# First attention of a Flamingo block: 16-bit planes of the probabilities transposed by DMA, split by GpSimd and joined by ScalarE

## The chip, the cores and the metric

One core of a Trainium2 chip runs the whole program. The metric is the device time of one execution in microseconds; lower is better.

## What is computed

The reference is a residual stack of four cross-attention layers and four feed-forward layers on `x` of 4 x 256 tokens x 256 features: Mamba, dense FFN, **first attention**, sparse experts, second attention, experts, quantised experts, chosen tokens. All of it is float32. The change concerns the first attention (the reference's `_L1_xattn_ref`), which for each of 4 batches and 16 heads of width 128 is

```
q = rms(xn @ Wq) * gq        # 256 x 128
k = rms(ctx @ Wk) * gk       # 256 x 128
p = softmax(q @ k.T / sqrt(128))      # 256 x 256
x = x + tanh(g) * (p @ (ctx @ Wv)) @ Wo
```

## The kernel before, in words

Every engine has its own program, written out in order; they meet at semaphores (`wait_ge`). The names used below are those of the code. The stages follow each other, and generators called `beside` put pieces of the next stage into a running one (`step(beside[...])`).

The first attention (`attention1_pe`, `_act`, `_dve`, `_pool`) runs over 64 **units**: unit u is one head of one batch. Units come in 32 **passes** N = u // 2, one head for two batches; passes 0 to 15 are the 16 heads for batches 0 and 1, 16 to 31 those for batches 2 and 3. The values are not projected: `a1_joined_pe` makes M = Wv Wo of a head once, the unit multiplies the probabilities with the raw context (`attend`), and then with M (`result`). K of passes 0 to 15 was projected earlier, during Mamba, so passes N below 16 project only Q.

For unit u TensorE does, in its own iteration u:

- `scores(u + 1)`, four 128 x 256 matmuls in two banks' halves (L1257; float32 matmuls appear as several records);
- in an even iteration `a1_turn_pe` for pass N + 1, eight transposes of Q and K (L1095);
- `transposed(u)`: four 128 x 128 transposes of the probabilities into PSUM bank 2 or 3 (L1268);
- even: `a1_project_pe` for K of pass N + 3 (L1074, from N + 3 = 16 on); odd, while N + 3 is below 16: `a1_joined_pe` (L1084);
- `attend(u - 1)` (L1277); even: the projection of Q (L1071); `result(u - 2)` (L1288).

ScalarE, in iteration u: scales the turned Q and K (L1131, even); waits for the transposes `a1_T` and copies them from PSUM to `PT` (L1343); squares or copies K's projection (L1107; L1115, L1116) or M (L1121); `exponentials(u + 1)` into `Pr`, two halves with their sums (L1331); squares and copies Q's projection (L1115, L1116). VectorE: the maxima of unit u + 1 (L1365, L1368), the inverse of the sums (L1374), the product copied to `Z` (L1380), the residual of `result` (L1389), then normalisation (L1155, L1158) or the sums of squares (L1142, L1144). GpSimd has one inverse root a pass (`a1_root_pool`, L1167), and in the second half the indirect scatters of the sorted experts' tokens (L1742), two at a step.

SP issues the loads: each pass's weights of 384 KB into one of two buffers (`attention1_sp`, L1053), and, between those of pass 19 and 20, the small tables and the 6 MB of weights of the sorted experts (`sorted_first_sp`, L1526 to L1531) and the second attention's weights (`a2_first_sp`). After the last pass's weights it goes on to the sorted experts' row loads (L1543).

The buffers matter for the waits. `Pr`, `PT` and `Z` have two places each, so work on unit u waits for the reader of unit u - 2:

```
        act.wait_ge(*at("a1_T", u))
        if u >= 2:
            act.wait_ge(*at("a1_A", u - 2))
        nc.scalar.copy(m.PT[:, w, :, :],
                       bank[2 + w].rearrange("p (t d) -> p t d", t=2)).then_inc(*tick("a1_PT", u))
```

## Time and profile before

| | us |
|---|---|
| median of 3 runs | 1067.0 (1062.03 to 1067.75) |
| the profiled execution, its own time | 1065.21 |
| its span, first to last instruction | 1063.9 |
| PE busy | 947.4 (89%) |
| DVE busy | 724.5 (68%) |
| ACT busy | 521.4 (49%) |
| POOL busy | 303.0 (28%) |
| mean granted TensorE clock | 0.947 of full speed |

The median and the profiled execution are different runs of the same program. Busy time is the union of an engine's instructions; waiting, semaphores and the issue of DMAs are not in it. PE is the row of matmuls and transposes, PEld that of weight loads, which overlap the matmuls; the first attention's units run from about 220 to 552 us of the span.

### The profile page before, as it was taken

What the parts mean: (1) busy time and instruction counts of PE and PEld (TensorE: products, weight loads), DVE (VectorE), ACT (ScalarE), POOL (GpSimd) and SP (SyncE); (2) the same over time, 40 slices, a digit from 0 to 9 for tenths busy, and PEclk for the clock granted to TensorE, in tenths of its full rate; (3) what the DMA queues carried; (4) which work ended last, traced back from release to release, by engine and by line L of the source; (5) the groups of instructions that cost most, each with busy time, mean ns of one, the idle gap of its engine ahead of it and who ended that gap; (6) DMA issues with size and microseconds to landing.
All of it is one profiled execution on the core that took longest, in us unless ns stands there. A gap on an engine that the chain in (4) does not pass through costs nothing.

```text
span 1063.9 us, 14909 instructions
## 1 busy us (share of the span) xinstructions
PE 947.4 (89%) x4814; PEld 678.0 (64%) x4814; DVE 724.5 (68%) x1877; ACT 521.4 (49%) x1346; POOL 303.0 (28%) x284
## 2 busy tenths in 40 slices
PE   7878789999999999999999989877788889988587
PEld 3323334567999998888977767754455546545475
DVE  5899894235777677678676445678798855667753
ACT  4665672135666666566644434354366542132331
POOL 3667692121111112155101424244312100011110
PEclk9888999999999999999999999999799999989689
DMA  9500001011111164122103436411100004202100
GB/s 362 227 0 0 1 0 50 1 30 44 35 43 46 45 231 156 31 66 90 45 1 119 160 119 198 129 65 51 50 1 2 1 3 156 75 31 61 55 20 20
DMA packets 28500, 75.00 MB, mean 70 GB/s; under 512 B 4092, under 2 KB 5382, under 8 KB 27656
## 3 DMA queue, kind: packets, MB, share of 16 engines
q1 hardware_dynamic: 24344, 63.81, 17.6%
q0 software_dynamic: 3072, 8.39, 2.5%
q10 hardware_dynamic: 1008, 1.86, 0.6%
q8 instruction: 39, 0.64, 0.3%
q14 instruction: 37, 0.30, 0.1%
HBM read 52.03 MB, written 22.02 MB: 70 GB/s over the span
## 4 chain that ended last, share of the span: by engine, by line
PE 63%; DVE 15%; issue 3%; ACT 2%; DMA 1%; SPq 1%; POOL 1%; DVEq 0%; POOLq 0%; ACTq 0%
PE psum L2195 5%; PE psum L1071 5%; PE psum L1796 5%; PE psum L1277 4%; PE psum L1288 4%; PE psum L927 4%; PE psum L1257 4%; PE psum L1268 2%; PE psum L938 2%; PE psum L2458 2%; PE psum L2816 2%; PE psum L1810 2%; PE psum L1095 2%; PE psum L2214 2%; PE psum L2834 2%
## 5 line engine op out<-in xcount | busy, mean ns | idle before, releaser
L1167 POOL TENSOR_TENSOR arena<-arena,mhalf 128x8 f32<-128x8 f32 x32 | 53.4, 1670 | 234.4 <-DVE arena L1144 234.3
L1389 DVE SCALAR_TENSOR_TENSOR X<-psum,arena,X 128x256 f32<-128x256 f32 x128 | 55.9, 478 | 65.0 <-PE psum L1288 64.9
L455 POOL TENSOR_TENSOR arena<-arena 128x512 f32<-128x512 f32 x64 | 82.7, 1317 | 6.0 <-DVE arena L855 3.9
L855 DVE TENSOR_TENSOR_SCAN arena<-psum,arena 128x512 f32<-128x512 f32 x64 | 74.7, 1209 | 9.1 <-ACT psum L711 8.0
L1331 ACT ACTIVATE arena<-psum,arena 128x256 f32<-128x256 f32 x128 | 59.9, 477 | 35.8 <-DVE arena L1368 33.4
L1796 PE MATMUL psum<-arena 128*128 x248 | 66.6, 391 | 10.7 <-DVE arena L1891 9.0
L2477 ACT ACTIVATE arena<-psum,arena 128x240 f32<-128x240 f32 x128 | 57.4, 463 | 33.7 <-DVE arena L2491 17.1
L545 PE MATMUL psum<-arena,ident 128*128 128x512 f32 x128 | 68.2, 658 | 0.1
L1288 PE MATMUL psum<-arena 128*128 128x256 f32 x256 | 65.9, 380 | 1.2 <-DVE X L1389 1.1
L1277 PE MATMUL psum<-arena 128*128 128x256 f32 x256 | 65.8, 380 | 0.0
L1257 PE MATMUL psum<-arena 128*128 128x256 f32 x256 | 65.8, 380 | 0.0
L1071 PEld LDWEIGHTS psum<-arena,xT 128*128 128x128 f32 x512 | 63.3, 196 | 3.9 <-issue 2.1
L1071 PE MATMUL psum<-arena,xT 128*128 128x128 f32 x512 | 64.1, 280 | 0.6 <-ACT arena L1131 0.6
L2195 PE MATMUL psum<-xT,arena 128*128 128x512 f32 x128 | 62.3, 628 | 1.3 <-ACT arena L3260 1.2
L1902 DVE COPY arena<-psum 128x256 f32<-128x256 f32 x62 | 26.1, 422 | 53.7 <-PE psum L1810 53.6
L241 POOL TENSOR_TENSOR rstd<-rstd,mhalf 128x4 f32<-128x4 f32 x14 | 14.7, 1052 | 161.5 <-DVE rstd L234 161.5
L1796 PEld LDWEIGHTS psum<-arena 128*128 128x128 f32 x248 | 42.7, 192 | 18.0 <-issue 14.4
L1343 ACT COPY arena<-psum 128x512 f32<-128x512 f32 x64 | 37.6, 588 | 33.7 <-PE psum L1268 33.7
L1257 PEld LDWEIGHTS psum<-arena 128*128 128x128 f32 x256 | 48.2, 190 | 6.6 <-issue 0.3
L2816 PE MATMUL psum<-ident,arena 128*128 128x128 f32 x256 | 39.2, 296 | 13.4 <-DVE arena L2965 5.4
L1288 PEld LDWEIGHTS psum<-arena 128*128 128x128 f32 x256 | 46.3, 190 | 7.0 <-issue 1.4
L1131 ACT ACTIVATE arena<-psum,cols 128x512 f32<-128x512 f32 x64 | 40.5, 685 | 19.6 <-PE psum L1095 19.5
(367 smaller groups left out, 2269.3 us busy)
## 6 DMA issues: line engine op xcount, KB each, us to landing
arena<-in_w SPq DMA_DIRECT2D x32, 384.0 KB, 3.1
tokens<-arena SPq DMA_DIRECT2D x2, 4096.0 KB, 22.6
arena<-tokens SPq DMA_DIRECT2D x32, 256.0 KB, 3.0
results<-arena SPq DMA_DIRECT2D x32, 256.0 KB, 2.0
arena<-in_moe SPq DMA_DIRECT2D x17, 384.0 KB, 3.0
arena<-in_moe SPq DMA_DIRECT2D x4, 1536.0 KB, 13.4
arena<-in_w SPq DMA_DIRECT2D x2, 1024.0 KB, 6.0
arena<-in_gu SPq DMA_DIRECT2D x1, 1280.0 KB, 7.2
```

The costliest lines, as they stand in the source:

```text
L455: nc.gpsimd.tensor_tensor(m.HC[:, v, :], m.Hs[:, v, :], m.Cs[:, s % 2, :], ALU.mult).then_inc(*tick("HC", s, c))
L545: nc.tensor.matmul(bank[m.bank_Y[h][c]], k.ident[:, :], m.HC[:, 2 * (s % 2) + c, :], start=False, stop=n == NSTATE - 1).then_inc(*tick("y_ ...
L855: nc.vector.tensor_tensor_scan(m.Hs[:, 2 * (s % 2) + c, :], bank[m.bank_dA[c]], input_of(m, s, c), 0.0, ALU.mult, ALU.add).then_inc(*tick( ...
L1071: mm = nc.tensor.matmul(bank[b][:, j * P:(j + 1) * P], k.xT[:, c, t * P:(t + 1) * P], m.W[:, p, c * P:(c + 1) * P], start=c == 0, stop=c = ...
L1257: mm = nc.tensor.matmul(bank[w][:, j * S:(j + 1) * S], m.Q[:, N % 2, i * S + j * P:i * S + (j + 1) * P], m.K[:, N % 2, i * S:(i + 1) * S], ...
L1277: mm = nc.tensor.matmul(bank[4][:, 0:S], m.ctok[:, 2 * m.batch(u) + c, :], m.PT[:, u % 2, c, :], start=c == 0, stop=c == 1)
L1288: mm = nc.tensor.matmul(bank[5][:, j * D:(j + 1) * D], m.Z[:, u % 2, j * P:(j + 1) * P], m.M[:, h, :], start=True, stop=True)
L1331: e = nc.scalar.activation(m.Pr[:, w, j, :], bank[w][:, j * S:(j + 1) * S], ACT.Exp, bias=m.nb[:, w, j:j + 1], scale=m.SCALE, accum_out=m. ...
L1796: mm = nc.tensor.matmul(bank[b][:, 0:D], m.xgT[:, n % 2, c, :], m.W[:, bass.ds(place + c * D, D)], start=c == 0, stop=c == DC - 1)
L2195: mm = nc.tensor.matmul(bank[b], m.W[:, slot, which, c * P:(c + 1) * P], k.xT[:, c, cols], start=c == 0, stop=c == DC - 1)
L2477: nc.scalar.activation(pr[:, a, 0:KM], v[:, a, 0:KM], ACT.Exp, bias=m.nb[:, u, a:a + 1], scale=m.SCALE, accum_out=m.sums[:, a % 2, places[ ...
L2816: mm = nc.tensor.transpose(bank[4 + w][:, c * S + j * P:c * S + (j + 1) * P], m.Pr[:, u, 2 * w + j, c * P:(c + 1) * P], k.ident[:, :])
```

## The change

Units 0 to 61 (`BY_DMA = 62`) no longer transpose their probabilities on TensorE. A float32 word is two 16-bit halves. GpSimd copies `Pr`, seen as uint16 by `planes`, into `halves`: all low halves, then all high ones. SP waits for that (`a1_H`) and for the reader of the same buffer, and issues one `dma_start_transpose` from `halves` to `turned`, eight blocks of 128 x 128 16-bit elements. ScalarE waits for it (`a1_D0`, `a1_D1`) and copies the planes back, interleaved, into `PT` (`joined_halves`), now after the exponentials of unit u + 1 and the Q projection and for unit u - 1. The last two units keep the old way (`turned`). `attend` and `result` come one unit later (u - 2, u - 3) on PE and on DVE. `Pr` has another order of columns. Weights: SP loads passes 0 to 4, ScalarE issues those of pass N + 5 at the end of odd iterations; it also issues the four 1.5 MB loads of expert weights at units 33, 37, 41 and 45 and the second attention's weights at unit 39. SP's row loads for the sorted experts come after the transpose of unit 61.

```diff
--- before.py
+++ after.py
...
@@ -1012,6 +1013,8 @@
     PASSES, UNITS = 32, 64
     SCALE = P ** -0.5
 
+    BY_DMA = 62
+
     def __init__(self, k):
         HD = self.HD
         k.at = 0
@@ -1021,7 +1024,7 @@
         self.R = k.place(3, 2, HT, HD)
         self.sq = k.place(2, HT, HD)
         self.ss, self.rr = k.place(3, 2, HT), k.place(3, 2, HT)
-        self.Pr, self.PT = k.place(2, 2, S), k.place(2, 2, S)
+        self.Pr, self.PT = k.place(2, 2, 2, P), k.place(2, 2, S)
         self.Z = k.place(2, S)
         self.ctok = k.place(NT, C)
         self.mx, self.nb = k.place(2, 2), k.place(2, 2)
@@ -1029,6 +1032,12 @@
         assert k.at <= KEYS1
         k.at = KEYS1
         self.Kr = k.place(HT, self.NH, HD)
+        k.at = 23856
+        self.halves = [k.place(2, 2 * S, dt=U16)]
+        self.turned = [k.place(2, 2 * S, dt=U16) for _ in range(2)]
+        assert k.at <= FIRST
+        k.at = LAST - 512
+        self.halves.append(k.place(2, 2 * S, dt=U16))
 
     @staticmethod
     def batch(u):
@@ -1042,17 +1051,34 @@
     eng.wait_ge(*k.s.at("HC", 31, 1))
 
 
-def attention1_sp(k, m, passes):
-    if passes[0] == 0:
-        mamba_left(k, k.sp)
-    for N in passes:
-        if N >= 2:
-            k.sp.wait_ge(*k.s.at("a1_P", N - 2, 1))
-            if N - 2 < m.NH:
-                k.sp.wait_ge(*k.s.at("a1_M", N - 2))
-        k.nc.sync.dma_start(m.W[:, N % 2, :], k.io["w1"][N % m.NH]).then_inc(*k.s.landed(f"a1_w{N % 2}", N))
-        if N == 0:
-            k.nc.sync.dma_start(m.ctok, k.io["ctok"]).then_inc(*k.s.landed("ctok_in"))
+def planes(v):
+
+    return v.bitcast(U16).rearrange("p (n h) -> p h n", h=2)
+
+
+def a1_weights(k, m, N, eng, queue):
+    if N >= 2:
+        eng.wait_ge(*k.s.at("a1_P", N - 2, 1))
+        if N - 2 < m.NH:
+            eng.wait_ge(*k.s.at("a1_M", N - 2))
+    queue.dma_start(m.W[:, N % 2, :], k.io["w1"][N % m.NH]).then_inc(*k.s.landed(f"a1_w{N % 2}", N))
+
+
+def attention1_sp(k, m):
+    mamba_left(k, k.sp)
+    a1_weights(k, m, 0, k.sp, k.nc.sync)
+    k.nc.sync.dma_start(m.ctok, k.io["ctok"]).then_inc(*k.s.landed("ctok_in"))
+    for N in range(1, 5):
+        a1_weights(k, m, N, k.sp, k.nc.sync)
+
+
+def a1_turned_sp(k, m, units):
+    for u in units:
+        k.sp.wait_ge(*k.s.at("a1_H", u))
+        if u >= 2:
+            k.sp.wait_ge(*k.s.at("a1_PT", u - 2))
+        k.nc.sync.dma_start_transpose(m.turned[u % 2].rearrange("p h (g i) -> p (h g) i", i=P),
+                                      m.halves[u % 2].rearrange("p h n -> p (h n)")).then_inc(*k.s.landed(f"a1_D{u % 2}", u))
 
 
 def a1_project_pe(k, m, N, q):
@@ -1266,7 +1292,7 @@
         for c in range(2):
             for j in range(2):
                 mm = nc.tensor.transpose(bank[2 + w][:, c * S + j * P:c * S + (j + 1) * P],
-                                         m.Pr[:, w, j, c * P:(c + 1) * P], k.ident[:, :])
+                                         m.Pr[:, w, c, j, :], k.ident[:, :])
         mm.then_inc(*tick("a1_T", u))
         k.free[2 + w] = [("a1_PT", u)]
 
@@ -1298,25 +1324,28 @@
             scores(u + 1)
         if first and N + 1 < m.PASSES:
             a1_turn_pe(k, m, N + 1)
-        transposed(u)
+        if u >= m.BY_DMA:
+            transposed(u)
         if first and N + 3 < m.PASSES:
             a1_project_pe(k, m, N + 3, 0)
         elif not first and N + 3 < m.NH:
             a1_joined_pe(k, m, N + 3)
-        if u >= 1:
-            attend(u - 1)
+        if u >= 2:
+            attend(u - 2)
         if first and N + 3 < m.PASSES:
             a1_project_pe(k, m, N + 3, 1)
-        if u >= 2:
-            result(u - 2)
+        if u >= 3:
+            result(u - 3)
         step(beside[u // 32])
+    attend(m.UNITS - 2)
+    result(m.UNITS - 3)
     attend(m.UNITS - 1)
     result(m.UNITS - 2)
     result(m.UNITS - 1)
     rest(beside[1])
 
 
-def attention1_act(k, m, beside):
+def attention1_act(k, m, beside, given):
     nc, act, at, tick, bank = k.nc, k.act, k.s.at, k.s.tick, k.bank
     table_act(k, ACT.Exp, "a1")
 
@@ -1324,24 +1353,34 @@
         w = u % 2
         act.wait_ge(*at("a1_nb", u))
         if u >= 2:
-            act.wait_ge(*at("a1_T", u - 2))
+            act.wait_ge(*at("a1_H", u - 2))
         if u >= 4:
             act.wait_ge(*at("a1_ri", u - 4))
         for j in range(2):
-            e = nc.scalar.activation(m.Pr[:, w, j, :], bank[w][:, j * S:(j + 1) * S], ACT.Exp,
+            e = nc.scalar.activation(m.Pr[:, w, :, j, :], bank[w][:, j * S:(j + 1) * S].rearrange("p (c k) -> p c k", c=2),
+                                     ACT.Exp,
                                      bias=m.nb[:, w, j:j + 1], scale=m.SCALE, accum_out=m.rs[:, u % 4, j:j + 1])
         e.then_inc(*tick("a1_E", u))
+
+    def joined_halves(u):
+
+        act.wait_ge(*at(f"a1_D{u % 2}", u))
+        if u >= 2:
+            act.wait_ge(*at("a1_A", u - 2))
+        nc.scalar.copy(planes(m.PT[:, u % 2].rearrange("p c i -> p (c i)")),
+                       m.turned[u % 2]).then_inc(*tick("a1_PT", u))
+
+    def turned(u):
+        act.wait_ge(*at("a1_T", u))
+        act.wait_ge(*at("a1_A", u - 2))
+        nc.scalar.copy(m.PT[:, u % 2, :, :],
+                       bank[2 + u % 2].rearrange("p (t d) -> p t d", t=2)).then_inc(*tick("a1_PT", u))
 
     exponentials(0)
     for u in range(m.UNITS):
         N, first, w = u // 2, u % 2 == 0, u % 2
         if first and N + 1 < m.PASSES:
             a1_turned_act(k, m, N + 1)
-        act.wait_ge(*at("a1_T", u))
-        if u >= 2:
-            act.wait_ge(*at("a1_A", u - 2))
-        nc.scalar.copy(m.PT[:, w, :, :],
-                       bank[2 + w].rearrange("p (t d) -> p t d", t=2)).then_inc(*tick("a1_PT", u))
         if first and N + 3 < m.PASSES:
             a1_projected_act(k, m, N + 3, 0)
         elif not first and N + 3 < m.NH:
@@ -1350,6 +1389,13 @@
             exponentials(u + 1)
         if first and N + 3 < m.PASSES:
             a1_projected_act(k, m, N + 3, 1)
+        if 1 <= u <= m.BY_DMA:
+            joined_halves(u - 1)
+        if u >= m.BY_DMA:
+            turned(u)
+        if not first and N + 5 < m.PASSES:
+            a1_weights(k, m, N + 5, act, nc.scalar)
+        given(u)
         step(beside[u // 32])
     rest(beside[1])
 
@@ -1401,15 +1447,17 @@
         if u + 1 < m.UNITS:
             maxima(u + 1)
         inverse(u)
-        if u >= 1:
-            attended(u - 1)
         if u >= 2:
-            result(u - 2)
+            attended(u - 2)
+        if u >= 3:
+            result(u - 3)
         if first and N + 2 < m.PASSES:
             a1_normalise_dve(k, m, N + 2)
         elif not first and N + 3 < m.PASSES:
             a1_sums_dve(k, m, N + 3)
         step(beside[u // 32])
+    attended(m.UNITS - 2)
+    result(m.UNITS - 3)
     attended(m.UNITS - 1)
     result(m.UNITS - 2)
     result(m.UNITS - 1)
@@ -1417,8 +1465,15 @@
 
 
 def attention1_pool(k, m, beside):
+    nc, pool, at = k.nc, k.pool, k.s.at
     for u in range(m.UNITS):
         N, first = u // 2, u % 2 == 0
+        if u < m.BY_DMA:
+            pool.wait_ge(*at("a1_E", u))
+            if u >= 2:
+                pool.wait_ge(*at(f"a1_D{u % 2}", u - 2))
+            nc.gpsimd.tensor_copy(m.halves[u % 2], planes(m.Pr[:, u % 2].rearrange("p c j k -> p (c j k)"))).then_inc(
+                *k.s.tick("a1_H", u))
         if not first and N + 3 < m.PASSES:
             a1_root_pool(k, m, N + 3)
         step(beside[u // 32])
@@ -1527,9 +1582,14 @@
     nc.sync.dma_start(m.upper, k.io["upper"]).then_inc(*k.s.landed("e_upper", tag))
     nc.sync.dma_start(m.consts, k.io["sort1"]).then_inc(*k.s.landed("e_consts", tag))
     nc.sync.dma_start(m.Wsh, k.io["moe1"][E]).then_inc(*k.s.landed("e_wsh", tag))
-    for g in range(0, E, 4):
-        nc.sync.dma_start(m.W[:, g * 768:(g + 4) * 768].rearrange("p (n w) -> p n w", n=4),
-                          k.io["moe1"][g:g + 4].rearrange("n p w -> p n w")).then_inc(*k.s.landed(f"e_wall{g // 4}", tag))
+
+
+def sorted_weights_act(k, m, g):
+
+    dense_left(k, k.act)
+    k.nc.scalar.dma_start(m.W[:, g * 768:(g + 4) * 768].rearrange("p (n w) -> p n w", n=4),
+                          k.io["moe1"][g:g + 4].rearrange("n p w -> p n w")).then_inc(
+                              *k.s.landed(f"e_wall{g // 4}", m.tag))
 
 
 def sorted_rows_sp(k, m, h, i):
...
+def a2_weights_act(k, m):
+    k.nc.scalar.dma_start(m.W, k.io["w2"]).then_inc(*k.s.landed("a2_w"))
...
@@ -3730,11 +3793,12 @@
     dense_sp(k, st.dense)
     sorted_zeros_sp(k, st.moe1)
     key_weights_sp(k, st.mamba)
-    attention1_sp(k, st.attention1, range(0, 20))
+    attention1_sp(k, st.attention1)
+    a1_turned_sp(k, st.attention1, range(32))
     dense_left(k, k.sp)
     sorted_first_sp(k, st.moe1)
     a2_first_sp(k, st.attention2)
-    attention1_sp(k, st.attention1, range(20, 32))
+    a1_turned_sp(k, st.attention1, range(32, st.attention1.BY_DMA))
     sorted_sp(k, st.moe1)
     sorted_left(k, k.sp, st.moe1)
     moe_first_sp(k, st.moe2, k.io["router2"], k.io["moe2"])
@@ -3768,6 +3832,14 @@
     rest(chosen_pe(k, st.chosen, 1, beside_quantised))
 
 
+def weights_act(k, m1, a2, u):
+
+    if u in (33, 37, 41, 45):
+        sorted_weights_act(k, m1, u - 33)
+    if u == 39:
+        a2_weights_act(k, a2)
+
+
 def scalar_program(k, st):
     m1, a2, ex, at2 = st.moe1, st.attention2, beside_experts, beside_attention2
     constants_act(k, st.mamba)
@@ -3776,7 +3848,8 @@
     dense_act(k, st.dense, 1, attention1_head_act(k, st.attention1))
     attention1_act(k, st.attention1, (
         head_act(k, "a1", 1, beside_attention1(0)),
-        later(2, begun(lambda: dense_left(k, k.act), sorted_head_act(k, m1, 0, beside_attention1)))))
+        later(2, begun(lambda: dense_left(k, k.act), sorted_head_act(k, m1, 0, beside_attention1)))),
+        lambda u: weights_act(k, m1, a2, u))
     sorted_act(k, m1, (both(shared_act(k, m1, 0, ex), sorted_head_act(k, m1, 1, ex),
                             later(KEYS, attention2_keys_act(k, a2, 0, ex))),
                        both(shared_act(k, m1, 1, ex), later(QUERIES, attention2_queries_act(k, a2, 0, ex, OVER)))),
```

## Rows read from the trace of the kernel before

**Rows 1.** The page: busy time by engine, and the chain that ended last by engine.

```profile
PE 947.4 (89%) x4814; PEld 678.0 (64%) x4814; DVE 724.5 (68%) x1877; ACT 521.4 (49%) x1346; POOL 303.0 (28%) x284
...
PE 63%; DVE 15%; issue 3%; ACT 2%; DMA 1%; SPq 1%; POOL 1%; DVEq 0%; POOLq 0%; ACTq 0%
```

**Rows 2.** Busy us by stretch: from:to length, PE, PEld, DVE, ACT, POOL; clock, DMA share, GB/s.

```profile
301.52:310.67 9.15, 9.15 (x60) 8.35 (x59) 6.64 (x17) 6.25 (x17) 1.64 (x1) 1.00 0.14 44
...
376.25:386.10 9.85, 9.85 (x66) 8.93 (x65) 6.59 (x16) 6.49 (x18) 1.64 (x1) 1.00 0.32 78
...
471.00:482.00 11.00, 10.53 (x68) 9.31 (x67) 8.88 (x23) 6.41 (x16) 6.68 (x6) 1.00 0.30 97
```

**Rows 3.** The chain of waits in an early and a late pass: start us, us, what.

```profile
308.43 0.44 PE psum L1268 x4
...
308.86 0.43 PE psum L1084 x2
...
377.94 1.13 PE psum L1074 x8
```

**Rows 4.** Groups of ACT by line and form: busy us, mean ns, then idle before.

```profile
L1343 ACT COPY arena<-psum 128x512 f32<-128x512 f32 x64 | 37.6, 588 | 33.7 <-PE psum L1268 33.7
...
L3260 ACT COPY arena<-psum 128x1024 bf16<-128x1024 bf16 x4 | 4.0, 1012 | 4.2 <-PE psum L3180 4.2
```

**Rows 5.** Timeline, DMA issues by SP and by ACT: start us, us, what.

```profile
383.07 0.43 SPq L1528 DMA_DIRECT2D arena<-in_sort  x1
...
1.14 0.45 ACTq L402 DMA_DIRECT2D cols<-in_cols  x1
```

**Rows 6.** Timeline of an early pass, all engines: start us, us, engine, line, operation.

```profile
301.71 1.03 PE L1257 MATMUL psum<-arena 128*128 128x256 f32 x4
...
303.21 1.27 ACT L1131 ACTIVATE arena<-psum,cols 128x512 f32<-128x512 f32 x2 [0.82 <-PE psum L1095]
...
304.20 1.64 POOL L1167 TENSOR_TENSOR arena<-arena,mhalf 128x8 f32<-128x8 f32 x1 [7.51 <-DVE arena L1144]
...
306.17 0.22 ACT L1331 ACTIVATION_READ_ACCUMULATOR arena<-psum,arena 128x1 f32 x1
...
307.40 1.03 PE L1257 MATMUL psum<-arena 128*128 128x256 f32 x4
...
308.39 1.28 DVE L1155 TENSOR_TENSOR arena<-arena 128x512 f32<-128x512 f32 x2
...
310.51 0.47 ACT L1331 ACTIVATE arena<-psum,arena 128x256 f32<-128x256 f32 x1 [0.65 <-DVE arena L1368]
```

**Rows 7.** Groups of POOL by line and form: one-input copies.

```profile
L2443 POOL COPY arena<-arena 128x512 f32<-128x512 f32 x8 | 5.1, 649 | 2.8 <-PE psum L2834 2.8
...
L440 POOL CAST arena<-arena 128x4096 bf16<-128x4096 f32 x1 | 3.6, 3597 | 0.0
```

**Rows 8.** Timeline of POOL in the second half: the scatters.

```profile
467.80 0.96 POOL L1742 DMA_INDIRECT tokens<-xn,arena  x1 [0.30 <-issue]
...
469.06 1.86 POOL L1742 DMA_INDIRECT tokens<-xn,arena  x1 [0.31 <-issue]
```

**Rows 9.** The page: DMA issues (KB each, us to landing) and the packets of queue q1.

```profile
results<-arena SPq DMA_DIRECT2D x32, 256.0 KB, 2.0
...
arena<-tokens SPq DMA_DIRECT2D x32, 256.0 KB, 3.0
...
q1 hardware_dynamic: 24344, 63.81, 17.6%
```

**Rows 10.** Timeline and busy us by stretch, where the weights of the next stages load.

```profile
408.62 0.97 PEld L1074 LDWEIGHTS psum<-arena,cT 128*128 128x128 f32 x8 [1.20 <-DMA arena<-in_w]
...
385.00:410.00 25.00, 24.04 (x157) 21.50 (x156) 18.25 (x48) 15.68 (x40) 3.53 (x3) 1.00 0.91 343
```

**Rows 11.** Busy us by stretch again: two later stretches with PE less busy.

```profile
760.00:800.00 40.00, 34.58 (x252) 23.30 (x249) 33.36 (x119) 23.42 (x87) 10.62 (x11) 1.00 0.01 1
...
985.00:1010.00 25.00, 14.17 (x69) 10.35 (x69) 18.62 (x52) 8.93 (x14) 4.52 (x5) 0.65 0.11 45
```

## What the change does to the time, predicted before any run of it

> **What bounds the kernel now.** I read the page first: TensorE is busy for 89% of the span, and the chain that ended last lies 63% on PE, 15% on DVE and 2% on ACT [rows 1]. The reader should see that only what shortens PE's own queue, or makes it wait, counts. The busy time by stretches then shows the first attention alone: in a pass (one head for two batches, two units) PE is busy for all of 9.15 us in the early form and all of 9.85 us in the late one, and ACT for 6.2 to 6.5 us, POOL for 1.64 us [rows 2]. Early passes are 0 to 12 (the keys come ready made); passes 13 to 28 also project K; 29 to 31 project nothing. The chain of an early pass holds nothing but PE pieces, the four transposes of a unit among them at 0.44 us; eight matmuls of the K projection are 1.13 us in a late one [rows 3]. In the second half, sorting work on DVE makes some passes longer: one stretch of 11.0 us has PE idle for 0.47 [rows 2].
>
> **What is removed.** Units 0 to 61 lose their PE transposes (L1268): 62 x 0.435 us (the piece is 0.44 rounded up, two of them 0.87) [rows 3] makes 27.0 us, all on the path. An early pass would take 8.28 us, a late one 8.98 us. ACT loses its copy of 512 columns out of PSUM, 0.59 us each [rows 4]. The wait for the PSUM bank goes too; next in line on PE is the wait for the joined probabilities.
>
> **What is added on ACT.** The join copies 1024 16-bit elements. The only row of that length is L3260, 1.01 us, from PSUM [rows 4]; the 512-column copy gives the lower end, 0.59 us, two such copies the upper end, 1.2 us. I take 1.01, the row nearest in length. Each pass also gets a weight DMA issued by ACT; SP needed 0.43 us for one issue, ACT 0.45 at the start of the kernel [rows 5]; its waits are for products which ACT's own previous steps already waited for, so I count 0.4. ACT is then busy 6.25 - 1.18 + 2.02 + 0.4 = 7.5 of 8.28 us: it fits, but it works in a fixed order, and the order costs something. Take the start of PE's even iteration (the scores, 301.71 in the timeline) as 0. ACT turns K and Q, squares, and does exponentials from 1.5 to 4.7 [rows 6], 0.5 less without the old copy; then the two projection copies, 1.1 us at 0.59 like L1343, a little overlapped, then the join of the odd unit, 1.0 us: ready at 6.3, when PE wants it at 5.25 (the even iteration, 5.69 long before, less 0.44) + 0.87 for the scores (twice L1084's work) + 0.43 for L1084 [rows 3] = 6.55 for the odd iteration's product. No wait so far. But the last exponentials of the pass start 3.11 us after the odd iteration (310.51 against 307.40 [rows 6], set by DVE's residual, normalisation and maxima), that is at 8.36; with 0.9 for them (two of 0.47), 1.0 for the join and 0.4 for the DMA, ACT is free at 10.7, 2.4 into the next pass instead of 1.5. That makes the odd unit's join 0.65 us late (7.2 against 6.55), and since a wait of PE also moves the next pass back, it settles at about half: 0.35 us a pass early, 0.5 late, where one more projection copy stands ahead (0.5) and PE's odd iteration comes without L1084. Returned: 13 x 0.35 + 16 x 0.5 = 12.6 us. Between a join of 0.59 us (nothing returned) and of 1.2 us (0.3 more a pass) this is 0 to 21 us.
>
> **What is added on POOL.** One copy of 1024 16-bit elements a unit. A 512-element copy took 0.65 us, a cast of 4096 took 3.60, 0.88 ns an element [rows 7]: between 0.9 and 1.3 us, I take 1.1. Two copies and the 1.64 us root are 3.8 us of a pass, hidden in POOL's idle 7.5 us; DVE's normalisation (308.39 to 309.67) lies between the two copies, and if one held the other back it would be by up to 1.1 us a pass, inside the range. But the copy of an even unit is queued behind that root, which waits for DVE's sums and ends 304.20 + 1.64 - 301.71 = 4.1 us into the pass [rows 6], though the exponentials were done 3 us before. In five or so passes two scatters stand ahead as well, 0.96 to 1.86 us each with 0.3 between them [rows 8]: 2.2 to 3.1 a pair, I take 2.6.
>
> **What is added on the DMA queue.** One transposing DMA a unit, 128 partitions x 2 KB = 256 KB, is in no row. The nearest are the plain 256 KB transfers: 2.0 us from issue to landing out of the arena, 3.0 us into it [rows 9]. The upper end: a transpose has to move 128 x 8 runs of 256 bytes; queue q1 spent 17.6% of 16 engines on 24344 packets, 0.123 us a packet [rows 9], so if each run cost a packet, 64 per engine are 7.9 us, with 1.5 us around it 9.4. From H (the split done) to ACT's go I take 3.0 + 0.4 for issue + 0.2 for two semaphores, L = 3.6 us; the ends are 2.2 and 9.4. Here the row and two pages differ. The Trainium skill says (Advanced Engine Details and Errata, X-Bar Transpose (TRN2)) that transposing DMAs are as fast as regular ones, which would leave L where the plain rows put it; but VectorE: DVE Perf Modes (The three transpose paths) gives 1309 ns for one 128x128 block of 16 bits, and eight such blocks one after another would be an estimate of 10.5 us. No row of this trace decides between them.
>
> What L must be: the even unit's split ends 4.1 + 1.1 = 5.2 us into a pass, and its product is due after scores and turn, each 0.87, 1.74 us (early) or 2.87 us (late, K's 1.13 more) into the next. So the pass is at least 5.2 + L + 1.0 - 1.74 = 4.5 + L early, 3.3 + L late, and 5.9 + L with scatters. At 3.6 that is 8.1, 6.9 and 9.5: nothing binds beyond the 8.6 and 9.5 us above. A late pass then gains 0.35 us, an early one 0.5.
>
> **What moves.** Weight loads leave SP for ACT (counted); the 6 MB of expert weights and the second attention's 768 KB leave SP's queue too and are spread over ACT's units 33 to 45. Before, they went out at once, and PE waited 1.2 us for the next head's weights behind them [rows 10]: -1.2 us. At 343 GB/s [rows 10] each 1.5 MB keeps the engines busy 4.6 us, and up to four transposes may land up to 2 us late; their slack takes most, I add 1 us. On SP, eight small loads of the next stages stand between the transposes of units 31 and 32: some 0.45 us of issue each [rows 5], 3.6 in all, against the 7 us between the odd unit's exponentials and the next even split: 0. The row loads of the sorted experts now stand behind the last transpose instead of inside the attention; they are due when attention ends, need 3.0 us and are issued some 7 us before it: 0. Products one unit later move the same PE work and let late exponentials be late by a unit: part of the sort's PE idle (five passes at the 0.47 us above, some 2.5 us) comes back, which the scatters' queue takes: 0 together.
>
> **Sum.** -27.0 + 12.6 - 1.2 + 1 = -14.6, against the profiled execution's own 1065.2 us (span 1063.9 and 1.3 around it): 1050.6 us. The median of the runs shown is 1067.0, 1.8 us above it, which gives 1052.
>
> **The clock.** It is granted in full (1.00, 2.4 GHz) in every stretch of the attention, and still 1.00 in a later stretch of 40 us with PE busy for 86% [rows 11]; it was 0.65 where PE was busy for 57%. Waits of half a microsecond in nine leave PE at 95%, so I charge nothing.
>
> **Rivals.**
> *The transpose lands too late (slower).* Place: PE's product of the even unit; price: each us of L over the limit is a us a pass; deciding point: L = 4.65 early (4.5 + L = 9.15), 6.5 late. At L = 6 early passes take 10.5 (+1.35 x 13 = 17.5), late ones still 9.5 (-0.35 x 11 = -4), five with scatters 11.9 against 10.5 (+7): +20, 1086 us. For it: the operation is unseen, and the queue behind the root is real. Against: plain transfers land in 2 to 3. Chance 0.17.
> *Each run costs a packet.* L = 9.4: early 13.9 (+62), late 12.7 (+31), scatter 15.3 (+24): 1065 + 117 = 1182 us. Chance 0.08. The Trainium skill's 1309 ns a block (VectorE: DVE Perf Modes, The three transpose paths) would end near there.
> *In between.* L from 4.5 to 5.5: early passes take 9.0 to 10.0 us, late ones still gain: 1059 to 1077 us. Chance 0.17.
> *PE gets it all.* If the join takes under 0.7 us or ACT's order leaves no lag, and the extra unit also takes the sort's stalls away: -27 - 1.2 - 2.5, 1035 us. Chance 0.08.
> Forecast: 0.50.
>
> **How the numbers follow.** This kernel's measurement can tell about 0.5% from no change, 5 us. Forecast and full gain are faster, with 0.03 of the in-between case: 0.61. The rest of that case: 0.09 within 0.5%, 0.05 above. Slower: 0.05 + 0.17 + 0.08 = 0.30. The likeliest case's own range, from the bounds of the join and the split, is 1040 to 1060. The range, 1034 to 1105, holds the full gain at the low end and reaches over the late landing up to L = 6.7 at the high end (+27, +2, +10.5: 1105), leaving the packet case and a little more out.
>
> **What would show it.** In the changed kernel: no PE transposes of the probabilities but for two units; early passes of about 8.6 us and late ones of about 9.5; PE idle ahead of L1277's matmuls, released by ACT's join; the join at 1.0 us, the split at 1.1. The landing of the transposing DMA decides: under 4.5 us the forecast holds. It is wrong if joins wait for the DMA rather than DVE or PE, if SP takes over 4 us to issue one, or if the granted clock falls in the stage.

## The result, and the profile after

The changed kernel is slower: 1092.3 us median of 4 runs (1091.66 to 1093.88), against 1066.4 us of the kernel before on the same chip; ratio 1.0243, 95% interval 1.0211 to 1.0275. The forecast was 1052 us and faster. The time lies inside the range given (1034 to 1105), the direction does not fit; that the range holds it is luck, since its upper end was made for a late landing, which did not come.

The page of the changed kernel, first busy time by engine, then the chain by engine, the packets of queue q1 and four groups of section 5 (busy us, mean ns of one, then idle time before it and who ended it). They answer to [rows 1], [rows 4], [rows 7] and [rows 9].

```profile
PE 935.4 (86%) x4566; PEld 654.3 (60%) x4566; DVE 731.4 (67%) x1877; ACT 560.3 (51%) x1346; POOL 367.7 (34%) x346
...
q1 hardware_dynamic: 83672, 62.37, 20.3%
...
PE 51%; DVE 16%; issue 8%; ACT 6%; POOL 4%; ACTq 0%; another core or an unknown queue 0%; POOLq 0%; DVEq 0%
...
L1303 PE MATMUL psum<-arena 128*128 128x256 f32 x256 | 72.7, 408 | 15.9 <-ACT arena L1370 15.8
...
L1370 ACT COPY arena<-arena 128x1024 uint16<-128x1024 uint16 x62 | 83.5, 1346 | 0.0
...
L1475 POOL COPY arena<-arena 128x1024 uint16<-128x1024 uint16 x62 | 65.0, 1060 | 16.6 <-ACT arena L1360 15.2
...
L1303 PEld LDWEIGHTS psum<-arena 128*128 128x128 f32 x256 | 45.2, 196 | 34.4 <-ACT arena L1370 30.4
```

PE did lose work (947.4 to 935.4 us busy) and its share fell all the same: it waits. The join (L1370) takes 1.35 us where 1.01 was assumed, the split (L1475) 1.06 where 1.1 was. The join's idle time is 0.0: in 62 joins ScalarE never waited for the DMA. That is the first large finding, since 42% of the forecast's chance was on a landing that decides.

The waits that grew (us in total, times, longest):

```profile
PEld psum L1303 <- ACT arena L1370: 30.4, 42, 1.3
...
PE psum L1100 <- ACT arena L1157: 18.2, 16, 2.8
...
PE psum L1303 <- ACT arena L1370: 15.8, 31, 1.1
```

There are two kinds. `attend` (L1303) waits for a join, as foreseen. The K projection (L1100) waits for ScalarE's copy of the turned Q and K (L1157): all 16 passes that project K show it, and the prediction has no such wait. The stretches that answer to [rows 2]: an early pass, a late one, and one where the sorting work is.

```profile
304.00:313.37 9.37, 9.04 (x52) 7.41 (x51) 6.57 (x17) 7.46 (x17) 3.60 (x3) 1.00 0.44 98
390.00:400.49 10.49, 9.24 (x57) 8.01 (x56) 6.61 (x16) 7.70 (x16) 3.66 (x3) 1.00 0.41 88
486.00:502.00 16.00, 12.51 (x59) 10.98 (x58) 9.87 (x28) 7.84 (x17) 7.75 (x8) 0.79 0.70 205
```

An early pass takes 9.37 us (9.15 before), a late one 10.49 (9.85 before). ACT is busy for only 7.5 to 7.7 us of them, so it isn't full; its order is what costs. The chain of waits through an early pass (start us, us, what):

```profile
307.49 2.04 PE psum L1097 x16
...
309.57 0.47 issue
310.04 0.58 ACT arena L1142
310.62 1.25 ACT arena L1370
...
311.91 1.13 PE psum L1303 x4
```

Here is the odd unit's join behind the two copies of the Q projection, the place that the prediction named. The groups of PE behind a wait are longer too: L1097 takes 2.04 us and L1303 1.13, where they take 1.78 and 0.86 in a queue without waits, since their first weight load is then in the open. The chain through a late pass is another one:

```profile
391.03 0.60 ACT arena L1360 x3
391.63 1.25 ACT arena L1370
392.87 0.56 ACT arena L1157
...
393.57 1.13 PE psum L1100 x8
...
397.35 0.88 PE psum L1314 x4
...
398.25 0.88 DVE X L1435 x2
399.13 1.13 DVE arena L1184
400.26 0.61 DVE arena L1411
```

It is a ring: exponentials, the **even** unit's join, the copy of the turned K out of PSUM bank 7, and only then the K projection, which is to write that same bank; then PE's products, VectorE's residual, normalisation and maxima, and the exponentials again. In a sorting pass VectorE is late in that ring, and PE idles longer (timeline of PE: start us, us, idle in brackets):

```profile
490.19 2.05 PE L1100 MATMUL psum<-arena,cT 128*128 128x128 f32 x8 [2.82 <-ACT arena L1157]
492.03 1.91 PE L1303 MATMUL psum<-arena 128*128 128x256 f32 x4
493.74 3.22 PE L1097 MATMUL psum<-arena,xT 128*128 128x128 f32 x16
496.79 1.03 PE L1314 MATMUL psum<-arena 128*128 128x256 f32 x4
```

After idling 2.8 us the same groups take nearly double: 2.05 us where 1.13 is usual, 3.22 for 2.02. The granted clock of this stretch is 0.79 of full speed, against 1.00 in a sorting stretch before the change [rows 2] and in the same 16 us of its span; the levels are 2.4 and 1.2 GHz. The wait is paid a second time.

### The profile page after: what moved, and what is told of

Its sections match the earlier page's. It is cut to its first block, busy times and chain, and to the rows that moved or that the text cites. A ratio compares the mean times of both kernels' runs of the same rounds, so it can differ in the third digit from the quotient of the medians.

```text
span 1090.3 us, 14647 instructions
## 1 busy us (share of the span) xinstructions
PE 935.4 (86%) x4566; PEld 654.3 (60%) x4566; DVE 731.4 (67%) x1877; ACT 560.3 (51%) x1346; POOL 367.7 (34%) x346
## 4 chain that ended last, share of the span: by engine, by line
PE 51%; DVE 16%; issue 8%; ACT 6%; POOL 4%; ACTq 0%; another core or an unknown queue 0%; POOLq 0%; DVEq 0%
PE psum L2255 5%; PE psum L1097 5%; PE psum L1856 5%; PE psum L928 4%; PE psum L1303 4%; PE psum L1314 2%; ACT arena L1370 2%; PE psum L939 2%; PE psum L1870 2%; PE psum L2521 2%; PE psum L2879 2%; PE psum L2274 2%; POOL tokens L1802 2%; PE psum L2897 1%; DVE arena L2555 1%
## 5 line engine op out<-in xcount | busy, mean ns | idle before, releaser
L1303 PE MATMUL psum<-arena 128*128 128x256 f32 x256 | 72.7, 408 | 15.9 <-ACT arena L1370 15.8
L1370 ACT COPY arena<-arena 128x1024 uint16<-128x1024 uint16 x62 | 83.5, 1346 | 0.0
L1097 PEld LDWEIGHTS psum<-arena,xT 128*128 128x128 f32 x512 | 65.1, 202 | 10.8 <-issue 9.6
L1475 POOL COPY arena<-arena 128x1024 uint16<-128x1024 uint16 x62 | 65.0, 1060 | 16.6 <-ACT arena L1360 15.2
L1097 PE MATMUL psum<-arena,xT 128*128 128x128 f32 x512 | 67.1, 287 | 3.6 <-ACT arena L1157 2.6
L1314 PE MATMUL psum<-arena 128*128 128x256 f32 x256 | 66.0, 380 | 1.3 <-DVE X L1435 1.1
L1303 PEld LDWEIGHTS psum<-arena 128*128 128x128 f32 x256 | 45.2, 196 | 34.4 <-ACT arena L1370 30.4
L1283 PE MATMUL psum<-arena 128*128 128x256 f32 x256 | 65.8, 380 | 0.0
```

The costliest lines, as they stand in the source:

```text
L1097: mm = nc.tensor.matmul(bank[b][:, j * P:(j + 1) * P], k.xT[:, c, t * P:(t + 1) * P], m.W[:, p, c * P:(c + 1) * P], start=c == 0, stop=c = ...
L1283: mm = nc.tensor.matmul(bank[w][:, j * S:(j + 1) * S], m.Q[:, N % 2, i * S + j * P:i * S + (j + 1) * P], m.K[:, N % 2, i * S:(i + 1) * S], ...
L1303: mm = nc.tensor.matmul(bank[4][:, 0:S], m.ctok[:, 2 * m.batch(u) + c, :], m.PT[:, u % 2, c, :], start=c == 0, stop=c == 1)
L1314: mm = nc.tensor.matmul(bank[5][:, j * D:(j + 1) * D], m.Z[:, u % 2, j * P:(j + 1) * P], m.M[:, h, :], start=True, stop=True)
L1370: nc.scalar.copy(planes(m.PT[:, u % 2].rearrange("p c i -> p (c i)")), m.turned[u % 2]).then_inc(*tick("a1_PT", u))
L1475: nc.gpsimd.tensor_copy(m.halves[u % 2], planes(m.Pr[:, u % 2].rearrange("p c j k -> p (c j k)"))).then_inc(*k.s.tick("a1_H", u))
```

## The experiments

Theory after the result: ScalarE's 1.35 us join stands in its fixed order ahead of things that PE needs. Rivals: the DMA's landing, GpSimd, the later products by themselves. The table holds all runs; its pass lengths are in us, from the timeline of each profiled execution, from the start of one group of Q and K transposes to the next: early is the mean of nine early passes, late of four late ones, rest the sum of the last 13 intervals, all the sum of the 31 intervals. Ratios are to the kernel before, timed beside each.

| kernel | median us | ratio (95%) | early | late | rest | all |
|---|---|---|---|---|---|---|
| before | 1062 to 1067 | 1 | 9.15 | 9.84 | 133.1 | 303.6 |
| changed | 1092.3 | 1.0243 (1.0211-1.0275) | 9.37 | 10.52 | 150.8 | 325.5 |
| e1_no_dma | 1096.5 | 1.0274 (1.0241-1.0308) | 9.49 | 10.63 | 151.0 | 327.4 |
| e2_high_join | 1072.1 | 1.0050 (1.0017-1.0084) | 8.69 | 9.77 | 144.8 | 308.8 |
| e3_all_pe | 1071.7 | 1.0036 (1.0016-1.0057) | 9.15 | 9.84 | 135.2 | 303.3 |
| e4_first_half | 1076.5 | 1.0079 (1.0060-1.0099) | 9.38 | 10.52 | 135.2 | 310.1 |
| e5_banks | 1065.7 | 1.0017 (0.9995-1.0039) | 9.05 | 9.67 | 136.9 | 300.2 |
| e6_pool_join | 1089.8 | 1.0258 (1.0235-1.0281) | 9.43 | 9.75 | 150.4 | 323.3 |
| e7_pool_first | 1073.9 | 1.0108 (1.0083-1.0134) | 9.44 | 9.86 | 135.3 | 309.6 |
| e8_pool_first_banks | 1059.0 | 0.9963 (0.9942-0.9984) | 8.60 | 9.56 | 135.3 | 294.8 |
| e9_early_banks | 1057.1 | 0.9934 (0.9916-0.9952) | 9.03 | 8.93 | 136.8 | 296.3 |
| e10_early | 1093.1 | 1.0275 (1.0251-1.0298) | 9.36 | 10.39 | 152.4 | 328.2 |
| e11_even_first | 1062.4 | 0.9998 (0.9978-1.0017) | 9.19 | 9.29 | 133.8 | 296.6 |
| **e12_both_first_root** | **1047.7** | **0.9854 (0.9824-0.9884)** | 8.27 | 8.73 | 127.6 | 279.2 |
| e13_first_root_old_banks | 1066.1 | 1.0028 (1.0005-1.0051) | 8.66 | 9.41 | 139.3 | 300.6 |
| e14_both_first | 1049.7 | 0.9871 (0.9825-0.9918) | 8.64 | 8.73 | 128.0 | 282.8 |

**Without the DMA.** The transposes are dropped; ScalarE joins the halves as they are (the probabilities stay untransposed), and GpSimd's split waits for the join of unit u - 2 in place of its DMA.

```diff
-        act.wait_ge(*at(f"a1_D{u % 2}", u))
+        act.wait_ge(*at("a1_H", u))
...
-                       m.turned[u % 2]).then_inc(*tick("a1_PT", u))
+                       m.halves[u % 2]).then_inc(*tick("a1_PT", u))
```

> No transposing DMA at all: the join reads the split halves directly as soon as they are split, so the products are of untransposed probabilities. Theory A (ScalarE's fixed order around a join of 1.35 us holds TensorE): the landing never mattered, so the time stays with the changed kernel, 1088 to 1096 us, early passes 9.37 us, late ones 10.5. Theory B (the transposing DMA lands late): faster, below 1085 us, with early passes under 9.1.

Measured 1.0274: nothing comes back. The passes even take 0.1 us more: in the chain of an early pass VectorE's L1414 takes 0.30 us where it takes 0.18 in the changed kernel, and it ends together with a GpSimd split (312.75 and 312.73 us), which now comes at another time. The landing of the DMA is no part of the loss. All landing rivals fall.

**A shorter join.** The join reads the high plane only, 512 elements (the low 16 bits of every probability are left out).

```diff
-        nc.scalar.copy(planes(m.PT[:, u % 2].rearrange("p c i -> p (c i)")),
-                       m.turned[u % 2]).then_inc(*tick("a1_PT", u))
+        nc.scalar.copy(m.PT[:, u % 2].rearrange("p c i -> p (c i)"),
+                       m.turned[u % 2][:, 1, :].bitcast(BF16)).then_inc(*tick("a1_PT", u))
```

> Split and DMA stay; the join copies the upper plane alone, 512 elements, read as bfloat16, so the lower 16 bits of the probabilities are left out. Theory A: the join falls from 1.35 to about 0.65 us and stands once in each pass's chain, so each pass gets 0.7 us shorter: early 8.6 to 8.7, late 9.8; 31 passes give -22 us, and some half-clock time goes too: 1064 to 1072 us. Theory B (DMA) or C (GpSimd's split is late): unchanged, 1088 to 1096 us.

The instruction by line, nanoseconds:

```profile
L1370 ACT CAST arena<-arena x62: 612/618/647, 254.3 to 552.7; 128x512 f32<-128x512 bf16 x62
```

0.73 us less a join takes 0.68 us from an early pass, 0.75 from a late one and 20 us from the time. The join lies on the path nearly whole, once a pass. With the short join the chain of an early pass holds PE alone and 0.13 us of waiting ahead of a Q projection of 2.02 us, where the bank's wait is; that of a late pass still has a join, 0.51 us. But even this shorter join leaves the kernel at 1.0050: its length alone is not the explanation.

**The order alone, and half of it.** `BY_DMA = 0` lets PE transpose every unit, products one unit later and loads as in the changed kernel; `BY_DMA = 32` does so from unit 32 on.

```diff
-    BY_DMA = 62
+    BY_DMA = 0
```

> All units transposed by TensorE as before, with the rest of the change kept: products one unit later, ScalarE issues the weight DMAs, expert weights spread. Theory A: the reordering by itself is worth -1 to -4 us (no 1.2 us wait for weights, less waiting for late exponentials), 1062 to 1066 us. Rival D (ScalarE's DMA issues or the later products cost by themselves): 1070 us or more.

> DMA transposes for units 0 to 31, TensorE for 32 to 63. By the passes of the two traces the second half holds some 17 of the 26 us (13 of them in five sorting passes with POOL's scatters, late exponentials and half-clock stretches), the first half 5: 1070 to 1075 us. If the loss were spread evenly over the passes: 1079 us.

The first is 1.0036, some 4 us, with the passes of before (303.3 us in all); theory A had expected a gain, and the figure is rival D's. About half of it is at the end: from the last Q and K transposes to PE's first product of the next stage's experts the trace has 15.6 us before, 17.7 here and 19.0 in the changed kernel. Products one unit later are one more unit to drain. Where the other half is, isn't shown. The second kernel (1076.5, expected 1070 to 1075, or 1079 with an even spread) has the steady passes of the changed one in its first half and those of PE in the second, and loses 4.6 us more: each half has its part, the larger one in the second (150.8 against 135.2).

**The bank.** K and Q of the running attention are projected into PSUM banks 2 and 3, which the PE transposes no longer need, instead of 7 and 6.

```diff
-            a1_project_pe(k, m, N + 3, 0)
+            a1_project_pe(k, m, N + 3, 0, 3)
...
-    b, p = 7 - q, N % 2
+    b, p = top - q, N % 2
```

> The changed kernel with one edit: the two projections of the running attention (K and Q of the next head) go to PSUM banks 2 and 3 instead of 6 and 7, so that PE's K projection no longer waits for ScalarE to empty the bank that the previous heads' normalised rows were turned in. Theory A (the even unit's join stands in ScalarE's order ahead of the copy that empties that bank, and PE's K projection waits for the bank): late passes fall from 10.5 us to 9.7 to 9.9, early passes stay at 9.4, and 16 late passes give back 0.5 to 0.8 us each: 1078 to 1085 us. Rival B (late passes are set by the joins themselves, through the exponentials that come after them, whatever the bank): late passes stay within 0.2 us of 10.5 and the time within 1088 to 1096 us. Rival C (the copy that empties the bank only hides another wait, for the product's join): late passes 10.1 to 10.4, 1086 to 1090 us.

Late passes fall to 9.67 us as theory A has it; but early ones fall as well (9.05), and the time by 24 us, where 7 to 14 were expected. The sorting passes gave most: the last 13 intervals lose 13.9 us. No wait of the K projection is left in this trace (18.2 us in the changed kernel), so late exponentials no longer hold it up.

**GpSimd joins.** The join goes from ScalarE to GpSimd, behind the next unit's split, and GpSimd's root behind the even unit's split; for all units, then for the first 32 alone, then for these with banks 2 and 3.

```diff
+        if 1 <= u <= m.BY_DMA:
+            pool.wait_ge(*at(f"a1_D{(u - 1) % 2}", u - 1))
...
+            nc.gpsimd.tensor_copy(planes(m.PT[:, (u - 1) % 2].rearrange("p c i -> p (c i)")),
+                                  m.turned[(u - 1) % 2]).then_inc(*k.s.tick("a1_J", u - 1))
```

> The changed kernel with the join moved from ScalarE to GpSimd, one iteration later there and behind the next split, and GpSimd's root sum of the next heads moved by one unit. Theory A (what costs is ScalarE's 1.35 us in its fixed order): early passes fall from 9.4 to 8.3 to 8.6 us, late passes of the first sixteen heads from 10.5 to 9.0 to 9.4; in the second half GpSimd then holds four copies of 1.06 us, a root of 1.6 and up to 5 us of scatters a pass, so that the sorting passes stay at 11 to 14: 1062 to 1076 us. Rival B (GpSimd is the tighter engine, its copies and VectorE's shut each other out): early passes no shorter than 9.2 us, and the time at or above 1085 us. Rival C (no transpose on PE is worth nothing because PE's clock falls or its weight loads are exposed): early passes at 8.9 to 9.2.

> As the run before, with GpSimd joining units 0 to 31 only; units 32 to 61 are transposed by PE as before the change, products still one unit later. Theory A: first sixteen heads as in the run before (12 early passes 0.6 to 0.8 us under the 9.15 of before the change, 4 late ones 0.4 to 0.8 under 9.85: minus 9 to 13 us), second half and end as in the kernel with PE transposes throughout and products one unit later (plus 4): 1055 to 1064 us. Rival B: no gain from the first half, 1069 us or more.

> As the run before, with the projections of the first half in PSUM banks 2 and 3. If the bank that the turned rows free is still waited for in the four late passes of the first half, this is 1 to 3 us under the run before; if with the join off ScalarE nothing waits for that bank any more, it is equal within 1 us. Either way the figure to compare with the kernel before the change: 1053 to 1063 us expected.

The first two miss theory A: with ScalarE rid of every join an early pass still takes 9.5 us. Both figures are those of rival B (GpSimd the tighter engine, or no gain), yet the third, with the same copies on GpSimd in the first half, shows that they do not set the 9.5 us. The time of the third lies in its range, the worth of the bank does not: it is 15 us there, where 1 to 3 were foreseen, and with the bank changed the early pass is 8.60. So the bank costs with no join on ScalarE at all. Chain of the second kernel:

```profile
303.87 2.54 DVE arena L1181 x2
...
308.27 1.17 ACT arena L1157 x2
...
309.57 2.02 PE psum L1097 x16
```

PE's Q projection starts when ScalarE has emptied the bank (L1157), and VectorE's normalisation (L1181) takes 2.54 us for two where the changed kernel has 1.29: GpSimd's copies lie beside it.

**The join's place.** The banks run, with the join ahead of the Q projection's copies in ScalarE's order; then the same edit in the changed kernel, with the old banks.

```diff
+        if 1 <= u <= m.BY_DMA:
+            joined_halves(u - 1)
         if first and N + 3 < m.PASSES:
             a1_projected_act(k, m, N + 3, 1, 3)
-        if 1 <= u <= m.BY_DMA:
-            joined_halves(u - 1)
```

> The kernel of the banks run (projections of the running attention in PSUM banks 2 and 3) with one more edit: in ScalarE's order the odd unit's join goes ahead of the two copies of the Q projection instead of behind them; nothing else moves. Theory A (two causes: the shared bank, taken away already, and the odd unit's join behind the projection copies, which in the banks run still set a pass: 0.47 + 0.58 + 1.25 us of ScalarE in its chain): early passes fall from 9.05 to 8.6 us, the figure that PE alone needs with GpSimd joining, late passes from 9.67 to 9.1 to 9.4; 12 x 0.45 + 10 x 0.4 us under the banks run: 1053 to 1058 us. Rival B (ScalarE is simply full: its work of a pass, some 8.0 to 8.6 us, sets 9.05 and 9.67 in whatever order): both pass lengths stay within 0.15 us and the time within 1062 to 1068.

> The changed kernel with the join's place alone moved ahead of the Q projection's copies, banks as in the changed kernel. If the two causes are one behind the other (the bank's emptying stands behind the even unit's join, which this does not touch), early passes stay at 9.2 to 9.4 us, late ones at 10.3 to 10.5, and the time is 1085 to 1092. If they add up, early passes fall to about 8.9 and late ones to 10.1: 1078 to 1084 us.

With the new banks late passes fall to 8.93 us, with the old ones next to nothing moves (10.39 for 10.52, and 1093.1 us, 1 us over the range of "one behind the other"): the bank's wait covers this one. Early passes stay at 9.03 us in the first kernel, against theory A, though the time, 1057.1, falls in its range. Its chain there:

```profile
304.69 0.60 ACT arena L1360 x3
305.29 1.24 ACT arena L1370
...
306.57 1.13 PE psum L1303 x4
307.70 1.78 PE psum L1097 x16
```

This L1303 stands just ahead of the Q projection, so it is the even unit's product: its join, at the end of ScalarE's odd iteration, follows exponentials that wait for VectorE. I had moved the odd unit's join, which only lay in the chain before.

**Joins ahead of the exponentials.** First the odd unit's alone, then both together with GpSimd's root behind the even split (the edit shown), each with banks 2 and 3; then this order and root with the old banks; then both joins first with banks 2 and 3 and the root at its old place.

```diff
+        if 1 <= u <= m.BY_DMA:
+            joined_halves(u - 1)
         if u + 1 < m.UNITS:
             exponentials(u + 1)
...
-        if not first and N + 3 < m.PASSES:
-            a1_root_pool(k, m, N + 3)
+        if first and N and N + 2 < m.PASSES:
+            a1_root_pool(k, m, N + 2)
```

> Projections in PSUM banks 2 and 3, and in ScalarE's even iterations the join of the odd unit ahead of the exponentials too, where ScalarE would otherwise wait for VectorE's maxima. Theory A (with the join between exponentials and Q copies the 9.03 us of an early pass are a ring: exponentials, join 1.24, product, projection, result, VectorE's residual, normalisation, maxima, and back; a join that runs while ScalarE waits for the maxima is out of it): early passes 8.55 to 8.7 us, late ones unchanged at 8.97 where PE's own queue is the chain, so 12 x 0.4 us under the run before: 1050 to 1055 us. Rival B (ScalarE full): early passes stay within 0.1 us of 9.03 and the time at 1056 to 1060. Rival C (the DMA lands after the join's new place): joins wait for the DMA by more than 0.3 us a pass, and early passes are 9 us or longer.

> As the run before, with the even unit's join ahead of the exponentials as well, and GpSimd's root sum of the heads' norms behind the even unit's split instead of ahead of it, so that this split no longer queues behind the root. Theory A (in the sorting passes PE waits 1.2 to 2.7 us for the even unit's join, because it stands behind exponentials that VectorE's sorting work makes late): these waits shrink, the seven longest passes of the second half lose 0.5 to 1.5 us each, steady passes stay at 8.6 and 8.97: 1044 to 1051 us. Rival B (the transposing DMA of the even unit lands only after the join's new place, some 3.5 to 4.5 us behind the split, and ScalarE then holds back the exponentials): joins idle for the DMA by over 0.5 us a pass, early passes 9 us or longer, and the time 1058 us or more.

> The changed kernel with both joins ahead of the exponentials in ScalarE's order and the root behind the even unit's split, and the projections left in PSUM banks 7 and 6 as in the changed kernel. Theory A (the order is the cause; the shared bank only passes on the lateness of a join that stands behind late exponentials): early passes 8.3 to 8.4 us, late ones 8.8 to 9.0, 1046 to 1055 us. Theory B (the bank is a cause of its own: the copies that empty it come in ScalarE's queue behind a join in any order, and PE's projections need it at once): early passes 8.6 or more, late ones 9.4 or more, the time 1060 to 1080 us.

> Banks 2 and 3, both joins ahead of the exponentials, but GpSimd's root ahead of the even unit's split as in the changed kernel. Theory A (the split that queues behind the root makes the even unit's DMA land some 4 us behind a split that ends 5.2 us into the pass, after the join's new place at about 7, and ScalarE holds back its exponentials for it): joins idle for the DMA by 0.5 to 2 us a pass, early passes 9.3 to 10.5 us, the time 1065 to 1095. Rival B (the root's place matters nothing, since the split is early enough): early passes 8.27 as in the run before, and 1044 to 1052 us.

The first is a miss of theory A (early passes 9.10 us once steady, 1062.4 us in all): the even unit's join still ends the ring. Late passes take 9.47 us, 0.50 more than the 8.97 that were to stay. The trace has the place (timeline):

```profile
378.54 1.04 POOL L1477 COPY arena<-arena 128x1024 uint16<-128x1024 uint16 x1 [1.33 <-ACT arena L1360]
378.94 1.72 DVE L1184 TENSOR_TENSOR arena<-arena 128x1024 f32<-128x1024 f32 x1
```

The normalisation L1184 lies in the chain of the late pass, and in this run it begins while GpSimd still splits: 1.72 us, against 1.22 in e9 and e12, where the split has ended by then. The second is the best kernel: 0.9854, 17 us under the banks run. The time is where theory A had it, the steady passes are shorter than it said (8.27 and 8.73 for 8.6 and 8.97). Its stretches, an early and a late pass:

```profile
304.00:312.28 8.28, 8.28 (x52) 7.56 (x51) 6.59 (x17) 7.58 (x17) 3.71 (x3) 1.00 0.52 113
385.00:393.74 8.74, 8.74 (x58) 8.07 (x58) 6.50 (x14) 6.76 (x16) 2.94 (x4) 1.00 0.79 217
```

PE is busy for all of a pass, early and late, while ACT has 7.58 us of work in the early one, no less than in the changed kernel. The 31 intervals are 24.4 us shorter than before the change and the time only some 15: from the last Q and K transposes to the experts' first product this kernel needs 20.4 us, 4.8 more than before. The other 4 us lie outside both, and no run looks into them. What more could be had is in the sort (timeline):

```profile
461.44 1.33 ACT L1370 COPY arena<-arena 128x1024 uint16<-128x1024 uint16 x1 [5.45 <-DMA arena<-arena]
462.82 2.08 PE L1303 MATMUL psum<-arena 128*128 128x256 f32 x4 [5.01 <-ACT arena L1370]
```

Here the landing does decide. Between 440 and 470 us the transposes land 3.1 us after issue at best, 5.2 at the median and 8.9 at worst. A load of 1.5 MB of expert weights was issued at 452.9, and GpSimd issued four scatters between 452.7 and 459.3; this passage has the longest wait. Which of them is the reason wasn't tried.

The third comes out as its theory B says, and answers what the bank does by itself. Its chain in an early pass, and PE's wait in the passes that project K:

```profile
316.32 0.02 issue
316.35 1.27 ACT arena L1157 x2
317.62 0.14 issue
317.76 2.02 PE psum L1097 x16
```

```profile
PE psum L1100 <- ACT arena L1157: 16.0, 16, 3.5
```

Early 8.66 us and late 9.41 against 8.27 and 8.73: 0.39 and 0.68 us a pass, and 18 us in the time (1.0028 against 0.9854). Where it comes from is seen beside the same place of a late pass in the kernel before (timeline):

```profile
386.31 1.04 PE L1095 MATMUL psum<-ident,arena 128*128 128x128 f32 x8
386.95 1.27 ACT L1131 ACTIVATE arena<-psum,cols 128x512 f32<-128x512 f32 x2 [0.46 <-PE psum L1095]
387.19 0.60 PE L1268 MATMUL psum<-ident,arena 128*128 128x128 f32 x4
387.75 0.97 PEld L1074 LDWEIGHTS psum<-arena,cT 128*128 128x128 f32 x8 [0.20 <-issue]
387.78 1.13 PE L1074 MATMUL psum<-arena,cT 128*128 128x128 f32 x8
```

Once the first half of the Q and K transposes is done, ScalarE (L1131 there, L1157 now) needs 0.02 + 0.70 + 0.14 = 0.86 us to give back bank 7 (the late chain of this run has these three pieces), and 0.02 + 1.27 + 0.14 = 1.43 for both banks. In the kernel before, PE had the other half of these transposes to do (0.42 us) and the four transposes of the probabilities (0.44) ahead of the K projection: 0.86, just enough for the bank and not for the next weights: PE's weight loads idle 0.20 us here, and the K projection takes 1.13 us [rows 3] where it takes 0.89 when no bank is waited for (chain of e9). The bank's wait was already to be seen. Take the 0.44 away and PE waits 0.44 and shows a weight load of 0.24: 0.68. In an early pass the product (0.86) stands there too: 1.43 - 0.42 - 0.86 = 0.15, and 0.24 again: 0.39. **The transposes that the change removed were the cover of another wait.**

Four of the kernels make a square, and it shows two causes of about the same size (ratios of the table):

| | old banks | banks 2 and 3 |
|---|---|---|
| joins behind the exponentials | 1.0243 | 1.0017 |
| joins first, root behind the split | 1.0028 | 0.9854 |

The bank is worth 24 us in the old order and 18 in the new one, the order 23 us with the old banks and 17 with the new ones. Either alone takes nearly all of the loss away; it needs both for the full gain.

The fourth kernel (e14) sides with rival B in the time (1049.7 us, the intervals of the two overlap) and with theory A in the trace: joins idle for the DMA for 53.7 us in place of 21.4, and every second early pass takes some 9.1 us instead of 8.27. The place behind the root costs about 3.6 us of the 31 intervals, and in the time 2 us, less than the runs can tell, not the 17 to 47 that A gave.

## Why the prediction was wrong

- **What is removed.** The 27.0 us of PE work are real: e12 has 8.27 and 8.73 us where 8.28 and 8.98 were to remain (late passes gain more, as their K projection too runs shorter in it, 0.89 us instead of 1.13). The step that failed is the sentence behind it: "The wait for the PSUM bank goes too; next in line on PE is the wait for the joined probabilities." Next in line was the wait for two other banks, 7 and 6, which the removed transposes had covered with nothing to spare. Without that wait the changed kernel is at 1.0017 instead of 1.0243: 24 of the 40 us that lie between forecast and result. It was to be read from the timeline of before: what stands on PE between L1095 and L1074, when L1131 ends, and that L1074 took 1.13 us.
- **What is added on ACT.** The join was mis-sized (1.35 us, above the upper end of 1.2), and the lag only half seen. That the odd unit's join stands behind the Q copies was right, and shows in the chain of the early pass. The even unit's join, right behind the last exponentials and ahead of the copy of the turned K, wasn't looked at: the sum puts the 1.0 us of that join on ACT and asks only how late it makes the odd one. So the second step that failed is the size of the term 12.6, given as 0 to 21: in e5, with the bank's wait gone, the 31 intervals are 3.4 us shorter than before the change where 27.0 were taken out, so 23.6 came back. The order alone is 17 us (e5 against e12), and with the shared bank 23. A part was in no term: a product that waits also shows its first weight load (1.13 us for 0.86), twice in an early pass of e5, 0.54 of the 0.77 us that it takes over 8.28. The 0.4 us for ACT's DMA issue was too much: L1064 (0.33 us at 304.04) lies beside exponentials that follow each other without a gap. That the busy time of ACT in an early pass came out as foretold, 7.5 us, is in part luck, since this term and the join were off in opposite directions.
- **What is added on POOL.** The size is right (1.06 for 1.1). The queue behind the root, taken as harmless, is harmless in the changed kernel, and costs about 3.6 us of the intervals in e14.
- **What is added on the DMA queue.** L was taken as 3.6 us, of which 3.0 from issue to landing; e12 shows 3.1 at the median. For the upper end the count of packets was about right (1024 expected, 1056 found for each transpose) and the 0.123 us for each was wrong; the 1.5 us around it come from no row. Queues q1 and q10 together went from 25,352 packets and 18.2% of the span to 90,824 and 26.0%, which is 65,472 packets more for 90 us more of 16 engines' time, 22 ns of one engine a packet. The Trainium skill's sentence that transposing DMAs are as fast as regular ones (Advanced Engine Details and Errata, X-Bar Transpose (TRN2)) agrees with the landing, 3.1 us against 2.0 and 3.0 of plain transfers [rows 9]; the landing does not bear out the estimate of 10.5 us for eight blocks one after another, from the Trainium skill's 1309 ns a block (VectorE: DVE Perf Modes, The three transpose paths). The three rivals on the landing answered a question that did not decide.
- **What moves.** Products one unit later were costed at nothing. The order with PE transposing costs some 4 us (e3), 2.1 of them seen at the end. That stalls of the sort would come back was wrong in sign: those passes cost most.
- **The clock.** "Waits of half a microsecond in nine leave PE at 95%, so I charge nothing": true for steady passes (1.00), false where a wait reached 2.8 us, with 0.79 over 16 us.
- **The sign.** The rival on the slower side had the time about right (1086) by a mechanism that didn't occur; that is luck. No rival had the mechanism that did.

## What to carry to other kernels

When work is taken off the engine that bounds, look at what it stood between: list, from the timeline, which waits of the next instructions ended while it ran, with their slack. Here a PSUM bank with no slack and a join in the wrong place turned 27 us of work saved into a loss of 26, and mending either one alone gives only a tie (1.0017, 1.0028). And when a longer step is put into an engine with a fixed order, look at what each instruction behind it frees, not only at who reads its result; a step whose input has been ready for long belongs where its engine would otherwise wait.

## What the runs showed of the hardware

- ScalarE's copy of 1024 16-bit elements within SBUF, with an interleaving write, takes 1.35 us, and a cast of 512 takes 0.62. A GpSimd copy of the split takes 1.06 and of the join 1.34 at the median of e7 and e8, up to 1.80 in e7 and 2.33 in e8.
- SP needs 1.23 us (median of 62 in the changed kernel) to issue one transposing DMA of 256 KB, against 0.43 for a plain load [rows 5].
- VectorE's tiny operations can stretch beside a GpSimd copy, and then end with it (timeline of the changed kernel):

```profile
475.19 1.36 DVE L1170 TENSOR_SCALAR arena<-arena 128x8 f32<-128x8 f32 x1
475.46 1.05 POOL L1475 COPY arena<-arena 128x1024 uint16<-128x1024 uint16 x1
...
484.79 1.30 DVE L1768 TENSOR_SCALAR arena<-arena 128x32 int32<-128x32 f32 x1
484.99 1.05 POOL L1475 COPY arena<-arena 128x1024 uint16<-128x1024 uint16 x1
```

L1170 takes 0.17 us at the median of its 32. Its longest in the kernel before, without splits, was 0.24. The normalisation L1181 takes 0.68 us at the median in the changed kernel and 1.14 in e8, where GpSimd copies twice as much in the first half, and L1184 1.22 us behind a split and 1.72 beside one (e9 and e11, above). By the Trainium skill (SBUF — State Buffer, Who interferes with whom) VectorE and GpSimd share a pair of ports, which one of them holds for a whole instruction, when VectorE's has two inputs in SBUF or runs in a mode that uses both its ports. These rows agree with that, but no run took a copy away and kept everything else, so the cause is read and not shown.
